# Gated delta-rule attention: who issues the loads of the inverses and keys, and the order of work in a slot

## What is computed

```python
q, k = l2norm(x@Wq)/4, l2norm(x@Wk); v = x@Wv; gate = x@Wg
beta = sigmoid(x@Wb); g = cumsum(-exp(A_log)*softplus(x@Wa + dt_bias))     # per chunk
L = tril(exp(g[:,None] - g[None,:]))
P = strict_tril((beta*k) @ k.T * L);  Ainv = I + P + P@P + ...              # the inverse
v = Ainv @ (beta*v);  kcd = Ainv @ (beta*k*exp(g))
for each chunk:                                                             # the scan
    v_new = v - kcd @ S
    o = (q*exp(g)) @ S + tril(q @ k.T * L) @ v_new
    S = S*exp(g_last) + (k*exp(g_last - g)).T @ v_new
o = rmsnorm(o)*norm_w * silu(gate);  x = x + o @ Wo
```

## Time and profile before

| | us |
|---|---|
| median of 3 runs | 1255.49 (1250.86 to 1259.27) |
| the profiled execution | 1255.64, its span 1253.8 |
| phase `delta` in it | from about 224 to 844 |

### The profile page before, as it was taken

How to read it: one execution, slowest core, us unless ns; L and a number is a source line. 1 busy time by engine, 2 the same in 40 slices (tenths; PEclk the granted TensorE clock), 3 DMA queues, 4 the chain that set the end, 5 groups by cost and what they waited for, 6 DMA issues and landing times. The chain is left out here.

```text
span 1253.8 us, 38504 instructions
## 1 busy us (share of the span) xinstructions
PE 1038.9 (83%) x15542; PEld 738.8 (59%) x15542; DVE 911.5 (73%) x2403; ACT 595.3 (47%) x1614; POOL 405.2 (32%) x580
## 2 busy tenths in 40 slices
PE   2999977676888888888888876669999798799978
...
GB/s 259 8 2 1 1 56 101 61 103 95 105 96 95 92 91 91 105 101 96 83 97 99 100 93 75 36 3 1 1 1 1 17 57 79 268 135 135 1 34 101
DMA packets 282624, 93.30 MB, mean 74 GB/s; under 512 B 208976, under 2 KB 275408, under 8 KB 282448
## 3 DMA queue, kind: packets, MB, share of 16 engines
...
...
## 5 line engine op out<-in xcount | busy, mean ns | idle before, releaser
L1764 DVE TENSOR_TENSOR delta_tmp<-delta_PR 128x130 f32<-128x130 f32 (+12 forms) x416 | 156.5, 376 | 9.1
L1761 DVE TENSOR_TENSOR delta_PR<-delta_PR,delta_tmp 128x130 f32<-128x130 f32 (+12 forms) x416 | 152.7, 367 | 9.4
L1615 ACT ACTIVATE delta_y<-psum 32x128 f32<-32x128 f32 x256 | 68.1, 266 | 82.9 <-PE psum L1450 80.7
L1854 POOL TENSOR_TENSOR delta_VK<-delta_QK,both_eg 128x256 f32<-128x256 f32 x32 | 20.9, 653 | 253.7 <-DVE delta_QK L1696 253.7
L1416 PE MATMUL psum<-delta_T,delta_pad 128*32 128x128 f32 x2048 | 81.5, 326 | 17.5 <-DMA delta_T<-inverse_scratch 17.4
L1416 PEld LDWEIGHTS psum<-delta_T,delta_pad 128*32 128x32 f32 x2048 | 69.5, 133 | 28.3 <-DMA delta_T<-inverse_scratch 22.4
L1360 PE MATMUL psum<-both_w_in,delta_xT 128*128 128x512 f32 x128 | 68.0, 656 | 20.2 <-DMA delta_xT<-turned_scratch 10.2
L1878 POOL TENSOR_TENSOR delta_S<-delta_E,delta_Bm 128x128 f32<-128x128 f32 x32 | 16.4, 514 | 205.2 <-issue 198.2
L1463 PEld LDWEIGHTS psum<-delta_y,delta_Kd 32*32 32x32 f32 x2048 | 23.3, 112 | 99.3 <-ACT delta_y L1615 99.3
L506 POOL TENSOR_TENSOR ffn_H<-ffn_hid,ffn_H 128x512 fp32r<-128x512 f32 x48 | 61.7, 1290 | 57.2 <-DVE ffn_H L472 57.2
L1631 ACT ACTIVATE delta_wide<-delta_S 32x128 f32<-32x128 f32 x256 | 78.1, 305 | 3.1
...
## 6 DMA issues: line engine op xcount, KB each, us to landing
within_scratch<-delta_PT SPq DMA_DIRECT2D x128, 64.0 KB, 1.9
...
delta_T<-inverse_scratch SPq DMA_DIRECT2D x128, 64.0 KB, 2.8
...
```

The source lines that it names most:

```text
L1615: i = a.activation(dst, heads(bank[6][rows, half * P:(half + 1) * P]), ACT.Copy)
L1761: i = v.tensor_tensor(after, after, t3, ALU.add)
L1764: i = v.tensor_tensor(t3, column.to_broadcast([P, j, n_after]), row.to_broadcast([P, j, n_after]), ALU.mult)
```

## The change

Six edits, all in or just ahead of `delta`:

1. The loads of the first two tiles of `delta_xT` are issued in phase `gates`, ahead of the last stores of that phase (`turned_in` is now a function of its own).
2. `inverse_in` is split: blocks 0 and 1 of each tile are loaded from SP's queue, at the places of before; blocks 2 and 3 from GpSimd's, those of both tiles in the even slot, between `fade_second` and `gate_o`. The wait for the landed write stands in `inverse_in`. `apply` waits for both.
3. `keys_in` goes from SP's queue to GpSimd's, last in its slot.
4. ScalarE: `keep_y` of the second half goes ahead of `root_qk`; `exp_decays` goes from before it to behind `sigmoid_g`; `keep_o` ahead of `spread_vk`; `root_o` to the end of the slot whose tile it belongs to.
5. VectorE: `scale_o` moves from the start of the next slot to the end of its own; `sum_o` from the end to ahead of `keep_within`; `scale_qk` from behind `keep_gate` to ahead of `own_heads` of the second half; `add_o` (with `new_stats`) goes last; the steps of `solve` are dealt out anew between them.
6. Two pairs of semaphores become one each (`u_ut`, `u_wt`; `s_e0`, `s_e1`), and the waits count both.

```diff
@@ -165,6 +165,7 @@
         phase_memory("binary", binary_memory).close()
         phase_memory("space", space_memory).close()
         late.close()
+        made["gates"].xT = made["delta"].xT
         B.gates_xn, B.ffn_xn, B.binary_xn = made["gates"].xn, made["ffn"].xn, made["binary"].xn
 
         def phase_end(eng, n):
@@ -980,6 +981,8 @@
         for k in range(KD):
             turned = bass.AP(tensor=B.xT_dram, offset=k * P * NT * P + b * 512, ap=[[NT * P, P], [1, 512]])
             e.dma_start(turned, M.XT[b % 2][k]).then_inc(S.xt_out[b % 2], 16)
+    for t in range(2):
+        turned_in(e, B, M.xT, S, t)
     taps_store(e, B, M, S)
     for ready, src, dram, part in ((1, M.g_hiT, B.g_dram, 0), (2, M.g_loT, B.g_dram, 1), (3, M.egT, B.eg_dram, 0)):
         e.wait_ge(S.a_g_rows, ready)
...
@@ -1264,16 +1267,33 @@
         stage(t, *more)
 
 
+def turned_in(e, B, xT, S, t):
+
+    b = t // BLK
+    e.wait_ge(S.xt_out[b % 2], 32 * (b // 2 + 1))
+    src = bass.AP(tensor=B.xT_dram, offset=t * P, ap=[[NT * P, P], [P * NT * P, KD], [1, P]])
+    e.dma_start(xT[t % 2].rearrange("p (k n) -> p k n", k=KD), src).then_inc(S.p_in[t % 2], 16)
+
+
+def inverse_in(e, B, M, S, t, blocks, done):
+
+    e.wait_ge(S.i_back[t // 2 % 2], 16 * (t // 4 + 1))
+    if t < 2:
+        e.wait_ge(S.zero, 1)
+    else:
+        e.wait_ge(S.u_mm, t - 1)
+    for q in blocks:
+        src = bass.AP(tensor=B.T_dram, offset=t * 65536 + q * 1024, ap=[[SUB, SUB], [4096, NH], [1, SUB]])
+        e.dma_start(blocks_of(M.T[t % 2], q), src).then_inc(done[t % 2], 16)
+
+
 def delta_sync(e, B, M, S, run):
     Pd, Td = B.P_dram, B.T_dram
 
-    def turned_in(t):
+    def rows_in(t):
         if t >= 2:
             e.wait_ge(S.p_vg, t - 1)
-        b = t // BLK
-        e.wait_ge(S.xt_out[b % 2], 32 * (b // 2 + 1))
-        src = bass.AP(tensor=B.xT_dram, offset=t * P, ap=[[NT * P, P], [P * NT * P, KD], [1, P]])
-        e.dma_start(M.xT[t % 2].rearrange("p (k n) -> p k n", k=KD), src).then_inc(S.p_in[t % 2], 16)
+            turned_in(e, B, M.xT, S, t)
 
     def decays_in(t):
         if t >= 2:
@@ -1292,18 +1312,6 @@
         dst = bass.AP(tensor=B.Kd_dram, offset=t * P * DM, ap=[[SUB, P], [SUB * P, 8], [1, SUB]])
         e.dma_start(dst, M.Kd_tok[t % 2].rearrange("p (n c) -> p n c", n=8)).then_inc(S.k_out[t % 2], 16)
 
-    def keys_in(t):
-
-        e.wait_ge(S.k_out[t % 2], 16 * (t // 2 + 1))
-        if t >= 2:
-            e.wait_ge(S.k_in[t % 2], 64 * (t // 2))
-        if t >= 7:
-            e.wait_ge(S.s_b, 2 * (t - 6))
-        for r in range(4):
-            src = bass.AP(tensor=B.Kd_dram, offset=t * P * DM + 8192 * r, ap=[[SUB, SUB], [1024, 8], [1, SUB]])
-            dst = M.Kd[t % 7][SUB * r:SUB * r + SUB, :].rearrange("p (n c) -> p n c", n=8)
-            e.dma_start(dst, src).then_inc(S.k_in[t % 2], 16)
-
     def pair_in(m):
         e.wait_ge(S.i_out[0], 64 * (m + 1))
         e.wait_ge(S.i_out[1], 64 * (m + 1))
@@ -1316,16 +1324,6 @@
         back = bass.AP(tensor=Td, offset=m * 131072, ap=[[1024, P], [1, 1024]])
         e.wait_ge(S.i_step, solve_count(m, 2 * HALF_SOLVE))
         e.dma_start(back, M.PR[m % 2]).then_inc(S.i_back[m % 2], 16)
-        e.wait_ge(S.i_back[m % 2], 16 * (m // 2 + 1))
-
-    def inverse_in(t):
-        if t < 2:
-            e.wait_ge(S.zero, 1)
-        else:
-            e.wait_ge(S.u_mm, t - 1)
-        for q in range(4):
-            src = bass.AP(tensor=Td, offset=t * 65536 + q * 1024, ap=[[SUB, SUB], [4096, NH], [1, SUB]])
-            e.dma_start(blocks_of(M.T[t % 2], q), src).then_inc(S.i_diag[t % 2], 16)
 
     def within_out(t):
         e.wait_ge(S.f_pt, t + 1)
@@ -1333,19 +1331,19 @@
             dst = bass.AP(tensor=Pd, offset=t * 65536 + r * 16384, ap=[[SUB, SUB], [1024, NH], [1, SUB]])
             e.dma_start(dst, M.PT[SUB * r:SUB * r + SUB, :].rearrange("p (n i) -> p n i", n=NH)).then_inc(S.i_out[t % 2], 16)
 
-    for n in range(-1, SLOTS):
-        at(turned_in, n + 1)
+    for n in range(SLOTS):
+        at(rows_in, n + 1)
         at(decays_in, n)
         at(keys_out, n - 1)
-        at(keys_in, n - 2)
         at(within_out, n - LAG_FORM)
         if n % 2 == 0:
             if 0 <= (n - 2) // 2 < NT // 2:
                 pair_in((n - 2) // 2)
-            at(inverse_in, n - 5)
+            if 0 <= n - 5 < NT:
+                inverse_in(e, B, M, S, n - 5, (0, 1), S.i_diag)
         elif 0 <= (n - 5) // 2 < NT // 2:
             pair_back((n - 5) // 2)
-            inverse_in(n - 5)
+            inverse_in(e, B, M, S, n - 5, (0, 1), S.i_diag)
 
 
 def delta_tensor(pe, B, M, S, run):
@@ -1403,11 +1401,11 @@
 
     def apply(t):
 
-        pe.wait_ge(S.i_diag[t % 2], 64 * (t // 2 + 1))
+        pe.wait_ge(S.i_diag[t % 2], 32 * (t // 2 + 1))
+        pe.wait_ge(S.i_late[t % 2], 32 * (t // 2 + 1))
         pe.wait_ge(S.u_pad, t + 1)
         if t > 0:
-            pe.wait_ge(S.u_ut, t)
-            pe.wait_ge(S.u_wt, t)
+            pe.wait_ge(S.u_w, 2 * t)
         for w in range(2):
             for g in range(G2):
                 for e in range(2):
@@ -1420,7 +1418,7 @@
     def from_values(t, half):
 
         if half == 0:
-            pe.wait_ge(S.u_ut, t + 1)
+            pe.wait_ge(S.u_w, 2 * t + 2)
         if t + half > 0:
             pe.wait_ge(S.s_bm, 2 * t + half)
         for s in range(2):
@@ -1434,7 +1432,7 @@
     def from_state(t, half):
 
         if half == 0:
-            pe.wait_ge(S.u_wt, t + 1)
+            pe.wait_ge(S.u_w, 2 * t + 2)
             if t == 0:
                 pe.wait_ge(S.zero, 1)
             else:
@@ -1593,14 +1591,14 @@
         a.wait_ge(S.u_mm, t + 1)
         if t > 0:
             a.wait_ge(S.s_ws, 2 * t)
-        a.activation(M.UT, bank[3][:, 0:DM], ACT.Copy).then_inc(S.u_ut, 1)
+        a.activation(M.UT, bank[3][:, 0:DM], ACT.Copy).then_inc(S.u_w, 1)
 
     def keep_wt(t):
 
         a.wait_ge(S.u_mm, t + 1)
         if t > 0:
             a.wait_ge(S.s_ws, 2 * t)
-        a.activation(M.WT, bank[3][:, DM:], ACT.Copy, scale=-1.0).then_inc(S.u_wt, 1)
+        a.activation(M.WT, bank[3][:, DM:], ACT.Copy, scale=-1.0).then_inc(S.u_w, 1)
 
     def keep_y(t, half):
@@ -1650,21 +1648,21 @@
     for n in range(SLOTS):
         Z = n - LAG_SCAN
         at(keep_y, Z, 0)
-        at(root_o, n - LAG_OUT)
         at(widen, Z, 0)
         at(squares, n)
         at(keep_kq, n - LAG_FORM)
+        at(keep_y, Z, 1)
         at(root_qk, n)
-        at(exp_decays, n - LAG_FORM)
-        at(keep_y, Z, 1)
         at(widen, Z, 1)
         at(keep_v, n)
         at(sigmoid_g, n)
+        at(exp_decays, n - LAG_FORM)
         at(keep_ot, n - LAG_OUT)
         at(keep_wt, n - LAG_APPLY)
         at(keep_ut, n - LAG_APPLY)
+        at(keep_o, Z)
         at(spread_vk, n - LAG_PAD)
-        at(keep_o, Z)
+        at(root_o, Z)
     a.wait_ge(S.f_rstd, NBLK + 1)
     a.wait_ge(S.p_qk, NT)
     a.wait_ge(S.p_vg, NT)
@@ -1773,12 +1771,12 @@
     def new_state(t, half):
         v.wait_ge(S.s_bm, 2 * t + half + 1)
         if half == 0:
-            v.wait_ge(S.s_e0, t + 1)
+            v.wait_ge(S.s_e, 2 * t + 1)
             if t > 0:
                 v.wait_ge(S.s_ws, 2 * t)
             v.tensor_tensor(M.X1, M.E0, M.Bm, ALU.subtract).then_inc(S.s_x, 1)
         else:
-            v.wait_ge(S.s_e1, t + 1)
+            v.wait_ge(S.s_e, 2 * t + 2)
             if t > 0:
                 v.wait_ge(S.s_wide, 2 * t - 1)
             v.tensor_tensor(M.S0[(t + 1) % 2], M.E1, M.Bm, ALU.add).then_inc(S.s_x, 1)
@@ -1804,34 +1802,32 @@
 
     for n in range(SLOTS):
         Z, O = n - LAG_SCAN, n - LAG_OUT
-        at(scale_o, O)
+        at(own_heads, Z, 0)
         solve(n, 0, 1)
-        at(own_heads, Z, 0)
-        solve(n, 1, 2)
         at(new_state, Z, 0)
-        solve(n, 2, 5)
+        solve(n, 1, 3)
         at(sum_qk, n)
-        solve(n, 5, 9)
+        solve(n, 3, 6)
         at(faded_q, n - LAG_FORM)
-        solve(n, 9, 14)
+        solve(n, 6, 10)
+        at(scale_qk, n)
+        solve(n, 10, 11)
         at(own_heads, Z, 1)
-        solve(n, 14, 15)
+        solve(n, 11, 12)
         at(new_state, Z, 1)
-        solve(n, 15, 18)
+        solve(n, 12, 15)
         at(keep_gate, n)
-        solve(n, 18, 20)
-        at(scale_qk, n)
-        solve(n, 20, 23)
+        solve(n, 15, 21)
+        at(sum_o, Z)
+        solve(n, 21, 24)
         at(keep_within, n - LAG_FORM)
-        solve(n, 23, 24)
+        solve(n, 24, 25)
         at(keep_attn, n - LAG_FORM)
-        solve(n, 24, 26)
+        solve(n, 25, 29)
+        at(scale_o, Z)
         at(add_o, O)
-        solve(n, 26, 27)
         if O < AHEAD * BLK:
             at(new_stats, O)
-        solve(n, 27, 29)
-        at(sum_o, Z)
 
 
 def delta_gpsimd(g, own, B, M, S, run):
@@ -1864,14 +1860,26 @@
             i = g.tensor_tensor(dst, src, factor.unsqueeze(3).to_broadcast([P, 4, 2, HD]), ALU.mult)
         i.then_inc(S.p_kd, 1)
 
+    def keys_in(t):
+
```

(25 more changed lines are left out.)

6 lines of the change are left out of this document (3 added, 3 removed).

## The result

| | us |
|---|---|
| before, median, timed together with the changed kernel | 1257.74 (1250.86 to 1264.64) |
| changed, median | 1248.78 (1242.54 to 1257.3) |
| ratio | 0.994, 95% interval 0.9922 to 0.9957 |
| span of the profiled executions | 1253.8 before, 1246.7 changed |

The change wins 0.6%, some 7.5 us by the ratio (the two medians lie 9.0 us apart), where 23.6 were forecast. The sign was right and the size was three times too large. The case "within 1%" is what happened, which I had given 24 in 100.

What follows compares the result with a forecast made beforehand. The prediction took VectorE to bound the attention's steady part, with TensorE close behind. Its sum was 1255.6 - 30.1 (waits) + 12.6 (GpSimd loads) - 4.5 (start) - 1.7 (end) = 1231.9, said as 1232 us; its case spans 1219 to 1241.

Steps and rivals of the forecast that it cites:

- within 1%: Whole kernel: the measured time differs from before by less than about 1%, 12.5 us; chance 0.24.
- the term of 30.1: Steady part: VectorE's waits at `scale_o`, `keep_gate` and half of `keep_within` go, 15.6 + 4.1 + 10.4 us won.
- Rival B: Steady part: `scale_o`'s 15.6 us of waiting come back at `keep_within` (L1713); 1247.5 us, 24 in 100.
- c: GpSimd's queue: the time one load holds the engine, taken as 0.9 us, the middle of 0.49 and 1.29.
- free point: Even slots: VectorE waits 4c - 2.55 us at `sum_o`, never below zero, so a load is free up to 0.64 us.
- Rival A: Even slots: loads hold GpSimd for long ahead of `gate_o`; the gain is gone at c = 1.39; 28 in 100.
- Start: Start of the attention phase: early first inputs and `scale_qk` win 8.4 us, the late exponential costs 3.9; 4.5 us won.
- End: End of the attention phase: `sum_o` no longer stands behind `add_o`; 1.7 us won, bounds 0 and 3.
- Order on VectorE and ScalarE: Steady part: with the new order nothing is added or removed, only waits can go; 30.1 us won.

Runs made afterwards that it cites:

- gate_first: The changed kernel with `gate_o` ahead of GpSimd's inverse loads instead of behind them: 1244.48 us, ratio 0.9912 to the kernel before.
- no_reads: The changed kernel with GpSimd's products `gate_o`, `decayed_k` and `kept_k` replaced by memsets that only write: 1232.01 us, ratio 0.9817 to the kernel before.
- exp_start: The changed kernel with the exponential back in its early place on ScalarE in the first four slots alone: 1244.10 us, ratio 0.991 to the kernel before.
- keys_on_sp: The changed kernel with the keys' loads back on SP's queue: 1248.64 us, ratio 0.9939 to the kernel before.

## Why the prediction was right or wrong

**Bound, and waits that go.** Right that VectorE bounds the steady part and which waits go. `scale_o`'s 15.6 and `keep_gate`'s 4.1 went to nothing; of `keep_within`'s 20.8 I had half stay and 2.7 stayed, so the term of 30.1 was in truth 37.8. Rival B (waits change their place to L1713) didn't happen, though its time, 1247.5, is the one nearest to the measured: a number that was met by another mechanism.

**What a load on GpSimd holds, c.** I took 0.9 us, the middle of two bounds. The upper one was misread: GpSimd's longest instruction in that trace is not the 1.29 us of the earlier trace rows but a memset of 1.80 us (L1846), and the middle would have been 1.15, at a cost of some 24 us.

```profile
L1287 POOL DMA_DIRECT2D delta_T<-inverse_scratch x64 | 41.5, 655 | 31.8 <-DMA inverse_scratch<-delta_PR 27.6 <-issue 4.1
...
L1873 POOL DMA_DIRECT2D delta_Kd<-key_scratch x128 | 74.7, 590 | 0.1
```

The inverse loads hold GpSimd 0.655 us each, the keys' 0.590. The formula's free point was 0.64, so the cost should have been 12 x (4 x 0.655 - 2.55) = 0.8 us, not 12.6. `sum_o` waits 8.2 us all the same, in 7 slots and not in 12, with or without `gate_o` ahead of the loads (9.2 in gate_first). Of it 6.2 us are in slots 8 and 32, where TensorE's granted clock, from one `sum_o` to the next, was 0.82 and 0.70 in the mean; the rest is in slots at 0.90 to 0.93, and no slot at 1.00 waits there. VectorE's own lateness hides part of the chain. In slot 14 the first `own_heads` ends at 429.18; the loads begin 2.9 us behind that and not 1.9, since the write landed later, but VectorE reaches `sum_o` at +11.4 and not +9.15, without waiting. In no_reads, where its work is shorter, the same place waits 27.8 us. How much of that is `gate_o` and how much `delta_T`, both late for TensorE, the runs don't tell apart: gate_first moved the one wait into the other. With the 4.9 us of `own_heads` the term came out at 13.1 us, which is near 12.6 by luck. Rival A's cause is refuted, as c is far from 1.39, though its sign showed: TensorE stood idle for `gate_o` 13 times, 1.9 us each. The Trainium skill (DMA: Bandwidth & Descriptors, Latency and other measured facts) gives about 1 us to the first byte for GpSimd against 0.6 for SP; here the median time from issue to landing of the same kind of load was 2.7 us on GpSimd's queue and 3.2 us on SP's (2.8 on SP's in the kernel before), so this difference didn't show.

**Start.** 4.5 us forecast, 5.9 measured (`sum_qk` of slot 6 at 291.00, before 296.93). The first projection came at 223.50, a little before I had it, and the second at 230.00, 8.6 us earlier than before, where I had 8.4. Of this 2.7 us were lost again up to slot 6, against my 3.9. The late exponential alone cost more than I worked out, 5.2 us by exp_start: TensorE waited for it five times, 10.7 us in all up to 303 us; in exp_start it is twice and 5.3 us. Other parts of the order gave some of it back.

**End.** 1.7 forecast, 0.6 measured from slot 31's `sum_qk` to the last `add_o`.

**The step that failed.** Under "Order on VectorE and ScalarE" I wrote that nothing is added or removed, only waits can go, and took every duration of VectorE as it was: longer instructions were a term put at nothing, without a reason. With the measured steady part the books are: -24.7 (waits, net of the new ones) + 20 (longer work) = -4.7, against the forecast's -30.1 + 12.6 = -17.5. The missing term is as large as the whole gain. The experiment sizes it apart from the books: with the products as memsets the change is worth 16.2 us, with them 7.5, so some 9 of the 16 us by which I was off. Of the rest no run gives a full account; one part lies behind the phase, which ends 9.8 us earlier while the profiled spans differ by 7.1. The lengthening could have been seen: in the earlier trace rows a step of 128x220 takes 0.39 us, and in the same slot of the same trace, beside `decayed_k` at 444.82, the next one takes 0.69:

```profile
445.07 0.69 DVE L1764 TENSOR_TENSOR delta_tmp<-delta_PR 128x228 f32<-128x228 f32 x1
```

The changed kernel's step of that shape, clear of GpSimd, takes 0.39. The price of an overlap was in the trace, and the change moves `gate_o`, `decayed_k` and `kept_k` against VectorE. The Trainium skill (SBUF — State Buffer, Who interferes with whom) says that a VectorE instruction with two SBUF inputs contends with a GpSimd instruction that reads the SBUF, and not with one that only writes it. The runs here agree: `own_heads`, with one operand in PSUM, takes 282 to 285 ns in the mean in every run, and with memsets for the products the work falls by 31.0 us.

**What stays open.** Do GpSimd's DMAs lengthen VectorE's instructions at all? The booking gives the inverse loads 5.8 us in the changed kernel, and 4.9 of them are in instructions that end less than 0.4 us before `gate_o` starts. With the same 64 loads it is 0.6 in no_reads, where a memset follows them, and 0.9 in gate_first, where `gate_o` stands ahead of them. So this share goes with the product and not with the loads. Whether the key loads lengthen anything is open: they have 3.9 us, and still 3.0 in no_reads, yet keys_on_sp, without any of them on GpSimd, did no less work. No run undoes the merged semaphores (edit 6) by themselves. And the phases behind the attention, whose code is the same, took 2.7 us longer in the changed kernel's profile (412.3 us against 409.6). There TensorE's granted clock was 0.93 against 0.95, and its same 2032 matmuls were busy 370.3 us against 367.1. The other profiles go the same way, 411.6 to 412.4 us at 0.93 and 410.4 to 411.9 at 0.94. Over whole runs the clock is lower too, 0.921 in the median against 0.930 before; no run tells why. VectorE's longer work isn't the clock's: from 310 to 760 it was 0.95 in both, and in no_reads, with less of VectorE's work than either, 0.94.
